# Graph attention over 4096 nodes: ScalarE's extra stages ahead of the value matmuls in steps with a plain block

## The reference, cut to what matters

```python
N, DIM, HEADS, DIM_FF = 4096, 128, 8, 512          # HEAD_DIM = 16
qkv = layer_norm(x, g1, be1) @ w_qkv
q, k, v = (qkv[:, 0], qkv[:, 1], qkv[:, 2])        # per head
scores = jnp.einsum('nhd,mhd->hnm', q, k) * SCALE
scores = jnp.where((adj != 0)[None], scores, -jnp.inf)
attn = jax.nn.softmax(scores, axis=-1)
out = jnp.einsum('hnm,mhd->nhd', attn, v).reshape(n, DIM)
x = x + out @ w_proj + b_proj
h2 = layer_norm(x, g2, be2)
return x + jax.nn.gelu(h2 @ w1 + b1) @ w2 + b2
```

## Time and profile before

| | |
|---|---|
| median of 3 runs | 1814.01 us (1806.6 to 1814.49) |
| the profiled execution's own time | 1812.5 us |
| its span on the core | 1810.7 us |
| mean granted clock of TensorE | 0.976 of full speed |
| busy, share of the span | PE 92%, DVE 78%, ACT 72%, POOL 65%, weight loads 31% |
| chain that ended last | PE 71%, ACT 15%, issue 10%, DVE 2% |

### The profile page before, as it was taken

How to read it: one execution, slowest core, us unless ns; L and a number is a source line. 1 busy time by engine, 2 the same in 40 slices (tenths; PEclk the granted TensorE clock), 3 DMA queues, 4 the chain that set the end, 5 groups by cost and what they waited for, 6 DMA issues and landing times.

```text
span 1810.7 us, 48122 instructions
## 1 busy us (share of the span) xinstructions
PE 1673.6 (92%) x17826; PEld 553.9 (31%) x17826; DVE 1421.2 (78%) x4495; ACT 1300.8 (72%) x1443; POOL 1179.4 (65%) x1113
## 2 busy tenths in 40 slices
PE   6989999999999999999999999999999999999985
PEld 3422222323223232323223232323223232233223
DVE  6888889877898779887888779887898778987601
ACT  4547777677776777777776877677776877777771
POOL 5944586568855787468855688458865688457441
PEclk9869999999999999999999999999999999999996
DMA  7710035202450035301360035300351024500000
GB/s 214 168 42 2 25 108 110 54 1 66 135 100 2 13 106 117 66 1 54 114 133 2 1 100 124 77 2 26 123 106 47 2 77 124 77 2 1 8 7 6
DMA packets 168846, 115.24 MB, mean 64 GB/s; under 512 B 139298, under 2 KB 149156, under 8 KB 168612
## 3 DMA queue, kind: packets, MB, share of 16 engines
q1 hardware_dynamic: 157860, 103.78, 23.7%
q10 hardware_dynamic: 10752, 8.39, 1.6%
HBM read 74.39 MB, written 4.19 MB: 43 GB/s over the span
## 4 chain that ended last, share of the span: by engine, by line
PE 71%; ACT 15%; issue 10%; DVE 2%; DMA 1%; POOL 0%; SPq 0%; ACTq 0%; DVEq 0%; POOLq 0%
PE pv_ps L1023 19%; PE ring_ps L960 14%; PE score_ps L1127 12%; PE score_ps L1112 12%; ACT probs L728 12%; PE score_ps L1046 2%; PE ring_ps L1080 2%; PE ring_ps L1071 2%; PE ring_ps L1056 2%; PE ring_ps L1062 2%; PE score_ps L1036 2%; PE score_ps L984 2%; ACT q_stack L612 1%; ACT hidden L689 1%; DMA adj_in<-adj 1%
## 5 line engine op out<-in xcount | busy, mean ns | idle before, releaser
L763 DVE CUSTOM_DVE_ANT_0 masked_out<-ring_ps,row_mask 128x512 bf16<-128x512 f32 x2048 | 1310.3, 687 | 163.2 <-PE ring_ps L960 129.4
L728 ACT ACTIVATE probs<-score_ps,score_scale 128x1024 f32<-128x1024 f32 x1024 | 1089.0, 1113 | 358.0 <-PE score_ps L1127 350.4
L517 POOL TENSOR_TENSOR probs<-probs,keep 128x1024 int32<-128x1024 int32 x256 | 604.4, 2362 | 324.3 <-ACT probs L728 313.3
L1023 PE MATMUL pv_ps<-probs,v_ones 128*17 128x512 f32 x4096 | 539.2, 599 | 0.5 <-POOL probs L517 0.4
L960 PE MATMUL ring_ps<-k_stack,q_stack 51*64 51x512 f16 x4096 | 493.3, 397 | 13.3 <-DVE row_max L763 12.8
L1127 PE MATMUL score_ps<-q_stack,k_stack 51*64 51x512 f16 x4096 | 373.5, 391 | 26.6 <-ACT probs L728 7.4
L1112 PE MATMUL score_ps<-mask_t,ident_bf 64*64 64x512 bf16 x3072 | 276.1, 387 | 60.9 <-ACT probs L728 14.6
L960 PEld LDWEIGHTS ring_ps<-k_stack,q_stack 51*64 51x64 f16 x4096 | 165.8, 104 | 454.7 <-DVE row_max L763 401.9
L1127 PEld LDWEIGHTS score_ps<-q_stack,k_stack 51*64 51x64 f16 x4096 | 116.9, 104 | 229.2 <-PE score_ps L1112 181.1
L763 DVE DVE_READ_ACCUMULATOR2_ANT row_max<- 128x1 f32 x2048 | 169.4, 83 | 0.0
L1112 PEld LDWEIGHTS score_ps<-mask_t,ident_bf 64*64 64x64 bf16 x3072 | 92.4, 105 | 211.3 <-ACT probs L728 114.1
(11 more groups left out here) (106 smaller groups left out, 969.6 us busy)
## 6 DMA issues: line engine op xcount, KB each, us to landing
adj_in<-adj SPq DMA_DIRECT2D x128, 512.0 KB, 4.1
xnT_dram<-attn ACTq DMA_DIRECT2D x8, 256.0 KB, 3.9
mask_t<-row_mask SPq DMA_TRANSPOSE x128, 3.4
xq<-xnT_dram ACTq DMA_DIRECT2D x8, 256.0 KB, 2.6
x_res<-x ACTq DMA_DIRECT2D x8, 256.0 KB, 4.4
out<-rows ACTq DMA_DIRECT2D x8, 256.0 KB, 2.6
w_sb<-L_gnn_w SPq DMA_DIRECT2D x2, 256.0 KB
probs<-x SPq DMA_DIRECT2D x1, 256.0 KB, 2.9
```

What stands on the lines that cost most here:

```text
L517: nc.gpsimd.tensor_tensor(view, view, keep[:, KEPT.index(m), :].unsqueeze(1).broadcast_to([128, 2, TILE]), ALU.mult).then_inc(probs_masked, 1)
L728: nc.scalar.activation(probs[:, (2 * g + n) % SLOTS, :], score_ps[:, half:half + 2, :].rearrange("p a n -> p (a n)"), ACT.Exp, scale=score ...
L763: nc.vector.tensor_tensor_reduce(out=masked_out[:, place % 3, :], in0=ring_ps[:, place % 3, :], in1=row_mask[:, j, ch * 512:(ch + 1) * 512 ...
L1023: last = nc.tensor.matmul(pv_ps[32 * k:32 * k + HD + 1, :], v_ones[:, block_of(g, b), 2 * p + a, :], probs[:, (2 * g + b) % SLOTS, a * TIL ...
```

## The change

```diff
-ACT_FILLS = {16: ("h2t", 0), 17: ("h2t", 1), 31: ("q", 0), 34: ("q", 1), 37: ("q", 2), 41: ("q", 3)}
+ACT_FILLS = {16: ("h2t", 0), 17: ("h2t", 1), 31: ("q", 0), 35: ("q", 1), 37: ("q", 2), 41: ("q", 3)}
...
                     for x in range(UNITS // 2, UNITS):
                         row(g, x)
+                    if g in act_fills and g % 2 == 1:
+                        act_fill(i, bcd, g, act_fills[g])
                     if g < LAG and d:
                         weigh_values(i - 1, made_by(i - 1), STEPS - LAG + g)
                     if g >= LAG and c:
                         weigh_values(i, bcd, g - LAG)
-                    if g in act_fills:
+                    if g in act_fills and g % 2 == 0:
                         act_fill(i, bcd, g, act_fills[g])
```

## The result

The changed kernel takes 1799.08 us (median of 9 runs, 1792.14 to 1803.3) against 1814.01 us (9 runs, 1806.6 to 1816.52). The ratio is 0.9918, 95% interval [0.9902, 0.9935]: 14.9 us faster, where 17 were forecast. Its profiled execution took 1803.26 us (span 1801.5), 4 us above that median.

What follows compares the result with a forecast made beforehand. PE, issuing in program order, was taken to bound the main loop. Per full tile 4.38 us saved less 2.08 added gave 2.30, in all 16.9 us off the profiled 1812.5: 1795.6, as a median 1797 us, range 1787 to 1806.

Steps and rivals of the forecast that it cites:

- What was removed: Stalls of masks behind fills: 0.95 us per up, 0.84 per q; 4.38 us saved per full tile.
- The first rival: Half the gain returns as PE's other waits, for exponentials and VectorE: 1806 us, chance 0.15.
- waits of L960 for VectorE or of L1112 for L728 grown by 8 us: Profile sign that rows wait longer for VectorE, or masks for exponentials, giving back half the gain: 1806 us, chance 0.15.
- What was added: New waits of moved fills for the first block's exponential, 2.08 us per full tile.
- 4 x 0.23: Steps 21, 23, 31 and 37: each moved fill waits 0.23 us for the exponential, per tile.
- 2 x 0.40: Steps 19 and 35: the copy delays the exponential, so each moved fill waits 0.40 us, per tile.
- second h2t, step 17: Moving this fill shortens step 18's masks, saving 0.30 us per tile; its own new wait costs 0.20.
- What costs nothing: GpSimd's q addition at step 36, later values, DMA, SP and VectorE's rows: no cost, over 1 us left for q.
- The sum: Per full tile 4.38 - 2.08 = 2.30 us; over all iterations 16.9 us, giving a median of 1797 us.
- q at step 35: q's second fill, moved from step 34: saves 0.39 us of stall, waits 0.40 for the exponential, per tile.

Runs made afterwards that it cites:

- the two halves: The change's two edits, each alone on the kernel before: fills ahead of values, 1800.95 us; q's second fill in step 35, 1814.73 us.
- the fill ahead of the rows: The change with odd-step fills one place earlier, ahead of the step's second pair of row units: 1822.53 us, ratio 1.0061 to the kernel before.
- the copy between the exponentials: The change with ScalarE's copy of the values in steps 19 and 35 moved between the two exponentials: 1796.05 us, ratio 0.9888 to the kernel before.
- the selective version: The change with fills ahead of values only in steps 19, 23, 25, 35, 41 (31 in tile 0): 1795.33 us, ratio 0.9893.
- short rows: The change with VectorE's row maximum over 384 of 512 columns: 1764.35 us, ratio 0.9736 to the kernel before.
- the order alone: The change with q's second fill back in step 34, behind the values: 1800.95 us, ratio 0.9925 to the kernel before.
- up alone: The kernel before with only the four up fills moved ahead of the values: 1799.82 us, ratio 0.9935.
- step 35 alone: The kernel before with q's second fill in step 35 instead of 34, all fills behind the values: 1814.73 us, ratio 0.9993.
- both: The change with fills ahead only where the next step stalled, and ScalarE's copy between the exponentials in steps 19 and 35: 1786.04 us, ratio 0.9865.
- before with short rows: The kernel before with VectorE's row maximum over 384 of 512 columns: 1777.92 us, ratio 0.9812.

## Why the prediction was right

**The mechanism.** Right, and shown: the stall behind a fill goes (the list of waits), a shorter one ahead of it comes, the order makes it and not the step of q (the two halves), and a longer wait of the fills turns the gain into a loss (the fill ahead of the rows).

**What was removed.** The stalls had the size that the starts gave. From step 24's first masks to its scores it was 607.52 - 606.09 = 1.43 us and is 603.99 - 603.52 = 0.47, so 0.96 is gone where 0.95 was forecast; steps 20 and 26 show the same, and step 42 shows 0.85 for 0.84. The idle in the row, 0.80 and 0.70, would have come nearer to the 0.79 and 0.62 that the pairs of 23 and of 41 show net of their forecast waits, but by chance. (The page of the skill that the prediction names speaks of how near a kernel is to its roofline; what bears on the length of a stall are these starts.) What failed is that nothing was put in the stall's place. The second rows of steps 18, 20, 24, 26 and 42 now take 0.51 or 0.52 us where they took 0.31 or 0.32: a wait for VectorE of 0.19 or 0.20, a fifth of a stall, and 6.7 us over the run. The first rival named this wait, at 8 us, half of the gain. Its sign, "waits of L960 for VectorE or of L1112 for L728 grown by 8 us", did not show it: the former grew from 12.8 to 14.1 us and the latter fell, since most of the new wait shows in no idle row.

That the total came close all the same is in part luck. The masks' waits for exponentials fell, which wasn't in the sum either: by the starts 0.16 us in steps 19 and 25 and 0.13 in steps 27 and 43, 4.1 us over the run.

**What was added.** "4 x 0.23" held in steps 23 and 31: the fill of step 23 starts 601.24 - 600.65 = 0.59 us after the second rows, where the values started 0.36 after them:

```profile
603.45 0.43 PE L960 MATMUL ring_ps<-k_stack,q_stack 51*64 51x512 f16 x4
```

"2 x 0.40" for steps 19 and 35 held too (0.41 and 0.44), and the copy between the exponentials gave 0.31 of it back; in steps 25 and 41 it is 0.14 where 0.08 was forecast. Two terms were not in the sum at all. In step 31 the sequence fill, values, down takes 0.20 us more than values, fill, down. In steps 21 and 37 the sequence with back takes less: values to back is 0.87 us (594.66 to 595.53) where fill to back took 1.06, so these pairs lose 0.10 and not 0.23. The forecast had "second h2t, step 17", "Saved: 0.30"; 0.26 came there, the second rows of step 18 now wait for VectorE, and the pair loses 0.11.

**What costs nothing.** Right. q at step 35 and GpSimd's addition at step 36 make no wait at step 37; ScalarE's reads of q come 0.21 us after the fill there as elsewhere, save where TensorE's clock is low.

**The sum.** 16.9 forecast, 14.9 measured, 15.9 in the profiles' loop without the clock's drops. The errors had both signs. The forecast was too high by 6.7 us for the waits for VectorE, which it left out, and by 1.2 for the sequence of step 31. It was too low by 4.1 us for the masks' waits, which it left out too, by 1.9 for steps 21 and 37, and by 1 for q at step 35. The medians also hold what the profile shows by chance, such as the clock below.

## What to carry to other kernels

Here TensorE issues in program order, and the best place that these runs found for a piece of work that another engine must take away was where the buffer has just come free: later, the next user of the buffer stalls for the taking; earlier, the issuer stalls for the freeing. Where other work already covered the taking (steps 21, 31 and 37), the earlier place only lost. Read both times off the timeline for each place in the loop, since here the same move gained 0.8 us in one step and lost 0.4 in another, and the selective version beat the uniform one. And look at what the freed engine meets next: a wait that goes is worth its length less the next wait in line, which may hide inside a busy row.

## What had not been expected of the hardware

**TensorE's clock drops at two steps of the loop.** In the change's profile TensorE runs at half of its full clock, 1.2 in place of 2.4 GHz, for some 3.4 us in three tiles, each time from the fill of step 37 on. The first of them in the stretches (length, busy times, PEclk):

```profile
645.00:650.00 5.00, 4.77 (x57) 2.19 (x50) 3.98 (x14) 4.17 (x6) 4.74 (x4) 1.00 0.21 72
650.00:653.40 3.40, 3.40 (x10) 0.59 (x14) 1.07 (x4) 1.97 (x3) 2.55 (x2) 0.50 0.41 147
653.40:656.00 2.60, 2.60 (x60) 1.39 (x52) 1.45 (x4) 0.37 (x1) 2.41 (x3) 1.00 0.00 0
```

and in the timeline, where the fill takes 1.97 us and not 1.12:

```profile
646.74 0.29 PE L927 MATMUL score_ps<-ident_h,max_part 128*2 128x128 f16 x4
646.95 1.05 PE L1056 MATMUL ring_ps<-sum_sel,attn 128*128 128x2 f32 x8
...
649.85 1.97 PE L1036 MATMUL score_ps<-xq,wq_rep 128*128 128x512 f32 x2 [0.15 <-ACT probs L728]
651.75 1.85 PE L1023 MATMUL pv_ps<-probs,v_ones 128*17 128x512 f32 x8
```

The pair of steps 37 and 38 takes 9.28 us with the drop and 7.63 in the next tile without it, so one costs 1.65 us. What TensorE did before the clock fell is alike each time: the shift transposes and the sums (two columns a matmul) at the end of step 36, step 37's scores, and a short idleness at the fill or just ahead of it, 0.15 or 0.16 us in nine of the twelve drops below, 0.27 with short rows and 0.58 with the fill ahead of the rows. Steps 20 and 21 have the same sequence with an up fill. Twelve such drops stand between 140 us and 1700 us in the six profiles in which the fill of step 21 or both it and that of step 37 go ahead of the values (3 in the change, 2 with the order alone, 3 with the copy between, 1 with up alone, 2 ahead of the rows, 1 with short rows), and all twelve begin at the fill of step 21 or 37. In the six profiles in which these two fills stand behind the values (before, step 35 alone, only where it stalled, both, behind in 21 and 37, before with short rows) there is none. That the place of the fill brings the drops about is what the kernel with just these two fills put back was to show, and its profile agrees. What they cost in a median is open: in the profiles that kernel's loop is 6.1 us shorter than the change's, 1.1 of it without the drops, but its median is the change's within the intervals, and profiles are one execution each. The Trainium skill, "TensorE: Matmul & The Clock Gate", Part 1, has the clock gated by how busy the array has been. The rows here agree in that the fall follows upon small matmuls and idleness, though PE's row is busy for 4.77 of the 5.00 us before it; which of the two brings it about no run separates.

**The start-to-start time of two groups depends on which group went before.** Down behind a fill starts 0.96 us after it and is followed by rows 0.99 us after its own start; behind values it takes 1.09 (rows above). Back behind the values comes 0.87 us after them, behind a fill 1.06 (597.25 to 598.31). These are differences of 0.1 to 0.2 us at a full clock with no idle time in any row, as large as the terms of the sum.
